# Early tiles in f16 parts, weight halves one expert at a time, a shorter GpSimd prologue, early gates by two transfers

## The chip, the cores and the metric

One NeuronCore of a Trainium2 chip runs the whole kernel. Its engines are TensorE (PE in the profile: matmuls, and PEld for the loading of their weights), VectorE (DVE), ScalarE (ACT), GpSimd (POOL) and SyncE (SP), which here only issues transfers. The metric is the device time of one execution in microseconds. Of the kernel before there are three timed runs, and one execution recorded by the hardware profiler.

## The reference

The block is a gated cross-attention followed by a gated mixture of experts, on 16 x 64 = 1024 tokens of 128 features.

```python
x = x + tanh(g_xattn[0]) * attention(ctx, ctx, layernorm(x), Wk, Wv, bv, Wq, bq, Wo, bo)
x = x + tanh(g_ffn[0]) * ffn(layernorm(x), gate_w, w1, b1, w2, b2)

def ffn(x, gate_w, w1, b1, w2, b2):             # 8 experts, 512 hidden, the best 2 per token
    probs = softmax(einsum('bsd,ed->bse', x, gate_w))
    topk_probs, topk_idx = top_k(probs, 2)
    oh = one_hot(topk_idx, 8)
    h = gelu(einsum('bsd,fed,bske->bskf', x, w1, oh) + take(b1, topk_idx))
    y = einsum('bskf,def,bske->bskd', h, w2, oh) + take(b2, topk_idx)
    return sum(y * topk_probs[..., None], axis=-2)
```

Attention is one head of 128 over 16 sequences of 64 keys. The 2048 choices (1024 tokens times 2) are what the second half of the kernel works through.

## The kernel before, in words

The program is written out by hand for five instruction streams, which meet only at semaphores. Inside a stream everything runs in the order in which it is written: an instruction that waits holds back all that stand behind it on its engine.

**Attention and routing.** The 1024 tokens are eight tiles of 128, taken in four groups of two. A table of times, `TIMES`, sorted into `ORDER`, sets in which order PE, DVE, ACT and POOL take the steps of the groups; the times serve only for sorting. For each group the router picks two experts per token, counts places and finds the row in DRAM to which each choice goes (`slots`). POOL then sends the rows, 16 indirect transfers in all (`send`, L417), into `rows_dram`, where every expert has a region of its own. Ahead of its first send, POOL works through a prologue of constants (L423 to L496).

**The expert tiles.** The choices are worked off in 20 tiles of 128 slots. Tiles 0 to 3 are the early ones: they hold the first 64 slots of each of the 8 experts, two experts to a tile, and don't come through DRAM. `one_hots` (DVE, L1051) builds selection matrices, `gather` (PE, L840) multiplies the normalised rows, split in two f16 halves, with them, and `copy_first` (ACT) takes the sum out. Tiles 4 to 7 are mixed: two experts each, looked up in a table that is made at run time. Tiles 8 to 19 hold one expert each. Tiles 4 to 19 are read back from `rows_dram` (SP, L396 and L402) once all sends have landed; `split_rows` (DVE, L1249 and L1251) splits them in f16 halves, `turn_rows` (PE, L879) transposes them, `copy_rows` (DVE, L1260) takes the result out of PSUM.

**One tile on PE.** `hidden(t)` multiplies with the first weights: early tiles in FP32 (L897), the others as three f16 products, high weights by high rows, high by low, and low by high (L900 to L902). `w1_hi` is made by ACT (`weights_hi`, L594), `w1_lo` by DVE (`weights_lo`, L1213). ACT takes the gelu (L666), and `output(t)` multiplies with the second weights in FP32 (L927). The order on PE is gather, output of the tile before, hidden for an early tile, and hidden(t), output(t - 1), turn_rows(t + 2) from tile 4 on.

**The end.** The results of tiles 0 to 15 go to DRAM by 16 indirect transfers of POOL in the order of the tiles (L510). For tiles 0 to 3 the gate is applied by ACT (`first_gated`, L620), which needs the tile's rows from DRAM for the gate's value and stands in ACT's stream behind the gelu of a later tile. When all 16 have landed, SP reads the results back (L406), and DVE and POOL add them up; tiles 16 to 19 are added by PE from a selection matrix. `keep_clock` (L688) is a run of matmuls that nobody reads, put where PE would otherwise be idle; `CLOCK_FILL` says how many stand where.

## Time and profile before

| what | value |
|---|---|
| three timed runs | 103.09, 103.31 and 103.7 us; median 103.31 |
| the profiled execution | 103.78 us |
| its span, first to last instruction | 102.0 us |
| mean granted TensorE clock | 0.922 of full speed |
| PE / DVE / ACT / POOL busy | 86.3 / 63.0 / 58.3 / 51.3 us |

The span is what the trace covers; the 1.78 us that lie around it are in the time and not in the trace. The busy times are sums over the whole span: no engine is busy throughout, and which one sets the pace changes from stage to stage.

### The profile page before, as it was taken

How to read it: one execution, taken by the hardware profiler on the slowest of the kernel's cores; microseconds unless marked ns; L12 is line 12 of the kernel's file. 1: busy time of each engine (PE TensorE's matmuls, PEld its weight loads, DVE VectorE, ACT ScalarE, POOL GpSimd, SP SyncE). 2: the span in 40 equal slices, each digit the busy share in tenths (PEclk: the TensorE clock that was granted, in tenths of full speed). 3: DMA queues.
4: the chain of work that ended last, by engine and by line, in shares of the span. 5: the costliest groups of instructions: out<-in, count | busy, mean ns of one | idle time of the engine just before them, and what ended most of it. 6: DMA issues, size and time to landing. Idle time of an engine off the chain costs nothing.

```text
span 102.0 us, 3022 instructions
## 1 busy us (share of the span) xinstructions
PE 86.3 (85%) x925; PEld 70.5 (69%) x925; DVE 63.0 (62%) x275; ACT 58.3 (57%) x193; POOL 51.3 (50%) x91
## 2 busy tenths in 40 slices
PE   5949888878996689999997789899999999999500
PEld 1445555743653459989986579778999999999500
DVE  2377759999888948996531202375468885527380
ACT  5356799849668811547666356956666574741000
POOL 6975698308777776740000000373577777700480
PEclk9999999999999855569999958999999999999995
DMA  2999996910111453860222245420110011128315
GB/s 36 328 420 431 431 431 241 289 42 26 55 52 52 124 140 107 249 246 13 58 38 45 52 103 124 90 71 18 40 34 18 26 42 58 46 53 278 113 55 151
DMA packets 11839, 13.32 MB, mean 131 GB/s; under 512 B 1475, under 2 KB 10327, under 8 KB 11568
## 3 DMA queue, kind: packets, MB, share of 16 engines
q1 hardware_dynamic: 10112, 10.59, 31.7%
q0 software_dynamic: 1024, 1.92, 5.8%
q10 hardware_dynamic: 688, 0.61, 2.2%
q8 instruction: 8, 0.13, 0.5%
q14 instruction: 7, 0.06, 0.2%
HBM read 9.03 MB, written 4.29 MB: 131 GB/s over the span
## 4 chain that ended last, share of the span: by engine, by line
PE 29%; POOL 20%; DMA 15%; issue 14%; DVE 12%; SPq 6%; POOLq 1%; ACT 1%; DVEq 0%
POOL dispatched L417 13%; PE bank L927 12%; DMA res<-results 5%; PE bank L900 5%; PE bank L902 4%; DMA x_sb<-in_x 4%; SPq L394 3%; PE bank L901 3%; SPq L396 3%; DMA dispatched<-rows,slot 3%; DMA results<-y_sb,in_rows 2%; POOL results L510 2%; PE bank L879 2%; DMA in_rows<-dispatched 2%; POOL rstd L454 2%
## 5 line engine op out<-in xcount | busy, mean ns | idle before, releaser
L666 ACT ACTIVATE hid<-bank,wp 128x64 f32<-128x64 f32 (+1 forms) x112 | 28.0, 339 | 19.8 <-PE bank L902 12.4
L510 POOL DMA_INDIRECT results<-y_sb,in_rows x16 | 16.2, 1013 | 27.1 <-ACT y_sb L620 23.4
L927 PE MATMUL bank<-w_sb,hid 128*128 (+2 forms) x192 | 23.3, 299 | 0.0
L417 POOL DMA_INDIRECT dispatched<-rows,slot x16 | 16.5, 1032 | 9.1 <-issue 8.2
L927 PEld LDWEIGHTS bank<-w_sb,hid 128*64 128x64 f32 (+1 forms) x192 | 19.9, 178 | 0.2
L900 PE MATMUL bank<-xs_t,w_hi 128*128 128x128 f16 (+1 forms) x80 | 13.9, 215 | 1.3 <-DVE xs_t L1260 1.3
L901 PE MATMUL bank<-xs_t,w_hi 128*128 128x128 f16 (+1 forms) x80 | 13.8, 213 | 0.0
L902 PE MATMUL bank<-xs_t,w_lo 128*128 128x128 f16 (+1 forms) x80 | 13.8, 212 | 0.0
L1260 DVE COPY xs_t<-bank 128x256 f16<-128x256 f16 x16 | 4.6, 290 | 14.2 <-PE bank L879 14.2
L688 PE MATMUL bank<-ones 128*128 128x512 bf16 x38 | 11.6, 423 | 1.2 <-DVE ones L995 1.2
L897 PE MATMUL bank<-xs_f,w_sb 128*128 128x64 f32 x64 | 9.7, 315 | 0.0
L900 PEld LDWEIGHTS bank<-xs_t,w_hi 128*128 x80 | 8.0, 101 | 2.2 <-issue 1.4
L897 PEld LDWEIGHTS bank<-xs_f,w_sb 128*128 128x128 f32 x64 | 9.1, 226 | 0.6 <-issue 0.5
L901 PEld LDWEIGHTS bank<-xs_t,w_hi 128*128 x80 | 8.0, 101 | 0.0
L902 PEld LDWEIGHTS bank<-xs_t,w_lo 128*128 x80 | 7.9, 100 | 0.0
L840 PE MATMUL bank<-hot,rows 128*128 128x128 f16 x64 | 6.2, 264 | 1.3 <-DVE hot L1051 1.2
L1249 DVE CAST parts<-in_rows 128x128 f16<-128x128 f32 x16 | 5.0, 313 | 3.8 <-DMA in_rows<-dispatched 3.8
L688 PEld LDWEIGHTS bank<-ones 128*128 128x128 bf16 x38 | 3.8, 111 | 4.3 <-issue 1.9
L840 PEld LDWEIGHTS bank<-hot,rows 128*128 128x128 f16 x64 | 5.3, 123 | 1.9 <-DVE hot L1051 1.0
L1213 DVE SCALAR_TENSOR_TENSOR w_lo<-w_sb,w_hi 128x512 f16<-128x512 f32 x8 | 5.0, 692 | 2.2 <-ACT w_hi L594 2.2
L569 ACT ACTIVATE rows<-x,nbias,rstd 128x256 f32<-128x256 f32 x8 | 4.4, 593 | 2.0 <-DVE nbias L1120 1.9
L1051 DVE TENSOR_TENSOR hot<-slot_no,pos 128x256 f16<-128x256 f32 (+1 forms) x12 | 5.4, 508 | 0.0
(198 smaller groups left out, 171.0 us busy)
## 6 DMA issues: line engine op xcount, KB each, us to landing
w_sb<-in_w SPq DMA_DIRECT2D x2, 2048.0 KB, 10.7
results<-zeros SPq DMA_DIRECT2D x1, 1024.0 KB, 5.7
w_second<-in_w SPq DMA_DIRECT2D x4, 256.0 KB, 4.3
res<-results SPq DMA_DIRECT2D x4, 256.0 KB, 5.0
in_rows<-dispatched SPq DMA_DIRECT2D x12, 65.0 KB, 2.0
dispatched<-pad_rows SPq DMA_DIRECT2D x9, 65.0 KB, 2.4
in_rows<-dispatched SPq DMA_DIRECT2D x16, 32.5 KB, 2.1
ctx_sb<-in_ctx_t SPq DMA_DIRECT2D x1, 512.0 KB, 4.9
```

The lines of the kernel that those rows point to most:

```text
L417: pool.indirect_dma_start(rows_dram, bass.IndirectOffsetOnAxis(ap=slot[:, t, k:k + 1], axis=0), rows[:, t, k, :], None).then_inc(sent, 16)
L510: pool.indirect_dma_start(results_dram, bass.IndirectOffsetOnAxis(ap=in_rows[:].bitcast(U32)[:, t, TARGET:TARGET + 1], axis=0), y_sb[:, t, ...
L666: mm = act.activation(hid[:, t % HIDS, b, part], hid_ps[h % len(hid_ps)][:, at + part.start:at + part.stop], ACT.Gelu_apprx_tanh, bias=b1[ ...
L688: pe.matmul(to[:, :], ones[:], ones[:, None, :].to_broadcast((P, 4, P)), start=True, stop=True)
L840: mm = pe.matmul(gather_ps[i % 2][:, 0:P], rows_16[:, t, c, :], hot[:, i, t, :, :], start=t == 0 and c == 0, stop=t == TILES - 1 and c == 1)
L897: mm = pe.matmul(to, w1_sb[:, e, f], xs_f[:, t, part], start=True, stop=True)
L900: pe.matmul(to, w1_hi[:, e, f], hi, start=True, stop=False)
L901: pe.matmul(to, w1_hi[:, e, f], lo, start=False, stop=False)
L902: mm = pe.matmul(to, w1_lo[:, e, f], hi, start=False, stop=True)
L927: mm = pe.matmul(to[part, :], hid[:, t % HIDS, b, part], weights, start=False, stop=b == BLOCKS - 1)
L1051: v.tensor_tensor(hot[:, i, a:b, :, :], slot_no[:, None, 2 * i:2 * i + 2, :].to_broadcast(shape), pos[:, a:b, 2 * i:2 * i + 2, None].to_br ...
L1213: v.scalar_tensor_tensor(to[:, q, :], at[:, q, :], WSCALE, hi[:, q, :], ALU.mult, ALU.subtract).then_inc(made_lo, 1)
```

## The change

The changed kernel makes these edits:

- The early tiles use the three f16 products too. `gather` writes the sums of the high and of the low halves into two pieces of PSUM, `copy_first` copies both as f16 (256 columns in place of 128), and `hidden` of an early tile waits for the low weights of its two experts.
- The high weights are made one expert at a time (eight copies of 512 columns in place of four of 1024), five of them further forward in the order; the low weights stand between the selection matrices instead of behind them all.
- On DVE the gates and slots of the last group stand before `locate`, `lanes` and `table` stand later, and the split of tile 6 stands behind the copies of tiles 4 and 5 instead of ahead of them.
- POOL's prologue loses nine instructions: numbers are used as integers where they were copied to FP32, and two pairs of comparisons become one each. The counting matmuls take f16 operands.
- The early tiles' rows from DRAM, needed only for gates and targets, come by two transfers behind tile 7's, in place of eight that took turns with tiles 4 to 7.
- `first_gated(t)` stands behind the gelu of tile t + 6 in place of t + 5.
- Three more matmuls of `keep_clock` follow the last group's ranks.

On DVE, once the last selection matrix of the first early tile is being made, these rows stand in the kernel before (`hot` is the selection matrices, `slot` the rows in DRAM of the last group, `b_16` and `w_lo` low halves of weights):

```order
L1130 SCALAR_TENSOR_TENSOR rows<-exps,tanhs,exp_rec 128x4
L1144 TENSOR_REDUCE slot<-place_k 128x4
L1033 SCALAR_TENSOR_TENSOR b_16<-b_in,b_16 32x128
L1051 TENSOR_TENSOR hot<-slot_no,pos 128x512
L1051 TENSOR_TENSOR hot<-slot_no,pos 128x256 x2
L1051 TENSOR_TENSOR hot<-slot_no,pos 128x512
L1051 TENSOR_TENSOR hot<-slot_no,pos 128x256 x2
L1051 TENSOR_TENSOR hot<-slot_no,pos 128x512
L1051 TENSOR_TENSOR hot<-slot_no,pos 128x256 x2
L1213 SCALAR_TENSOR_TENSOR w_lo<-w_sb,w_hi 128x512 x8
```

In the changed kernel the same stretch of DVE's stream reads (`tile_row`, `tile_experts`, `sel` and `tile_rows` are the table of the further tiles):

```order
L1020 SCALAR_TENSOR_TENSOR b_16<-b_in,b_16 32x128
L1198 SCALAR_TENSOR_TENSOR w_lo<-w_sb,w_hi 128x512 x2
L1037 TENSOR_TENSOR hot<-slot_i,pos 128x512
L1037 TENSOR_TENSOR hot<-slot_i,pos 128x256 x2
L1169 SCALAR_TENSOR_TENSOR tile_row<-bank,place_i 1x20
L1170 TENSOR_SCALAR tile_experts<-bank 1x20
L1172 TENSOR_SCALAR sel<-bank,lane_less 128x20
L1174 TENSOR_SCALAR tile_rows<-tile_row 1x20
L1198 SCALAR_TENSOR_TENSOR w_lo<-w_sb,w_hi 128x512 x2
L1037 TENSOR_TENSOR hot<-slot_i,pos 128x512
L1037 TENSOR_TENSOR hot<-slot_i,pos 128x256 x2
L1198 SCALAR_TENSOR_TENSOR w_lo<-w_sb,w_hi 128x512 x2
```

The slots of the last group have left this stretch (they stand 14 rows ahead of `b_16` now), the table has come into it, and each early tile now has two low weights behind its selection matrices.

Further on in DVE's stream of the kernel before, the first rows from DRAM are split (`parts`, first tile 4, then 5, then 6) and copied (`xs_t`):

```order
L1213 SCALAR_TENSOR_TENSOR w_lo<-w_sb,w_hi 128x512 x8
L1249 CAST parts<-in_rows 128x128
L1251 TENSOR_TENSOR parts<-in_rows,parts 128x128
L1249 CAST parts<-in_rows 128x128
L1251 TENSOR_TENSOR parts<-in_rows,parts 128x128
L1249 CAST parts<-in_rows 128x128
L1251 TENSOR_TENSOR parts<-in_rows,parts 128x128
L1260 COPY xs_t<-bank 128x256 x3
```

In the changed kernel this place on DVE reads:

```order
L1198 SCALAR_TENSOR_TENSOR w_lo<-w_sb,w_hi 128x512 x2
L1238 CAST parts<-in_rows 128x128
L1240 TENSOR_TENSOR parts<-in_rows,parts 128x128
L1238 CAST parts<-in_rows 128x128
L1240 TENSOR_TENSOR parts<-in_rows,parts 128x128
L1246 COPY xs_t<-bank 128x256 x2
L1238 CAST parts<-in_rows 128x128
L1240 TENSOR_TENSOR parts<-in_rows,parts 128x128
L1246 COPY xs_t<-bank 128x256
```

The copies of tiles 4 and 5 no longer stand behind the split of tile 6.

The diff, cut to what the edits above rest on:

```diff
-LAG = 2
+LAG, LATER = 2, 2
+FIRST_LOADS = 4
...
-    W1_HIGH: [14.9],
+    W1_HIGH: [14.9, 14.91, 22.2, 23.6, 28.0, 33.0],
...
-              (RANKS, 2): 2, (X1_T, 3): 3, (ROUTE, 3): 6, (RANKS, 3): 3}
+              (RANKS, 2): 2, (X1_T, 3): 3, (ROUTE, 3): 6, (RANKS, 3): 6}
 W1_LOW_EARLY = 1
-HIGH_PARTS = 4
+HIGH_PARTS = 8
...
-            def load_shared(t):
-                for i in range(2):
-                    half = slice(i * PART, (i + 1) * PART)
-                    if t < EARLY:
-                        at = FIRST_ROW + (2 * t + i) * REGION
-                        sp.dma_start(in_rows[half, t, :], rows_dram[at:at + PART, :]).then_inc(loaded[t], 16)
-                    else:
-                        sp.dma_start(in_rows[half, t, :], rows_dram[bass.ds(first[2 * (t - EARLY) + i], PART), :]).then_inc(loaded[t], 16)
-
-            for t in range(EARLY, SHARED):
-                load_shared(t)
-                load_shared(t - EARLY)
-            for t in range(SHARED, N_TILES):
-                sp.dma_start(in_rows[:, t, :], rows_dram[bass.ds(first[2 * MIXED + t - SHARED], SLOT_TILE), :]).then_inc(loaded[t], 16)
+            regions = rows_dram[FIRST_ROW:PAD_ROW, :].rearrange("(t i r) w -> i r t w", i=2, r=REGION)
+            for t in range(EARLY, N_TILES):
+                if t == EARLY + FIRST_LOADS:
+                    for i in range(2):
+                        sp.dma_start(in_rows[i * PART:(i + 1) * PART, 0:EARLY, :], regions[i, 0:PART, :, :]).then_inc(loaded_first, 16)
+                for part, i in entries(t):
+                    sp.dma_start(in_rows[part, t, :], rows_dram[bass.ds(first[i - EXPERTS], part.stop - part.start), :]).then_inc(loaded[t], 16)
...
-            pool.tensor_copy(slot_no[:], slot_i[:]).then_inc(numbers_set, 1)
...
-            pool.tensor_copy(past[:], past_i[:]).then_inc(numbers_set, 1)
-            pool.tensor_scalar(second[:], lane_i[:], EXPERTS - 0.5, float(EXPERTS), ALU.is_gt, ALU.mult).then_inc(numbers_set, 1)
-            pool.tensor_copy(lane_f[:], lane_i[:]).then_inc(numbers_set, 1)
-            pool.tensor_copy(place_no[:], place_i[:]).then_inc(numbers_set, 1)
-            pool.tensor_copy(edge[:], edge_i[:]).then_inc(numbers_set, 1)
-            pool.wait_ge(numbers_set, 9)
-            for i in range(2):
-                pool.tensor_scalar(after[:, i, :], past[:], EXPERTS * i + 0.5, None, ALU.is_gt).then_inc(numbers_set, 1)
-                pool.tensor_scalar(same[:, i, :], past[:], float(EXPERTS * i), None, ALU.is_equal).then_inc(numbers_set, 1)
-            pool.tensor_tensor(seg_expert[:], lane_f[:], second[:], ALU.subtract).then_inc(numbers_set, 1)
-            pool.tensor_scalar(seg_first[:], second[:], 2.0 * WHOLE / EXPERTS, None, ALU.mult).then_inc(numbers_set, 1)
-            pool.wait_ge(numbers_set, 15)
+            pool.tensor_scalar(after[:], past_i[:], 0.5, None, ALU.is_gt).then_inc(numbers_set, 1)
+            pool.tensor_scalar(same[:], past_i[:], 0.0, None, ALU.is_equal).then_inc(numbers_set, 1)
+            pool.tensor_scalar(seg_first[:], lane_i[:], EXPERTS - 0.5, 2.0 * WHOLE, ALU.is_gt, ALU.mult).then_inc(numbers_set, 1)
+            pool.wait_ge(numbers_set, 3)
+            pool.tensor_tensor(seg_expert[:], lane_i[:], seg_wrap[:], ALU.add).then_inc(numbers_set, 1)
+            pool.wait_ge(numbers_set, 7)
             pool.tensor_scalar(seg_row[:], seg_expert[:], float(REGION // PART), float((FIRST_ROW + PART - PAD_ROW) // PART), ALU.mult, ALU.add).then_inc(numbers_set, 1)
             pool.tensor_scalar(seg_less[:], seg_expert[:], -float(EXPERTS), None, ALU.add).then_inc(numbers_set, 1)
...
-                act.activation(xs_f[:, t, :], gather_ps[t % 2][:, 0:P], ACT.Copy).then_inc(first_ok, 1)
+                act.activation(xs_first[:, t, :, :], gather_ps[t % 2][:, 0:2 * P].rearrange("p (c s) -> p c s", c=2), ACT.Copy).then_inc(first_ok, 1)
...
-                act.wait_ge(loaded[t], loads_of(t))
+                act.wait_ge(loaded_first, 32)
...
-            weights_hi(w1_hi, w1_sb, ld_w1, w1hi_ok, 1)
+            weights_hi(w1_hi, w1_sb, ld_w1, w1hi_ok, 6)
...
-                if t in (1, 2):
-                    weights_hi(w1_hi, w1_sb, ld_w1, w1hi_ok, t + 1)
+                if t == 1:
+                    weights_hi(w1_hi, w1_sb, ld_w1, w1hi_ok, 7)
...
-                if EARLY + 1 <= t < 2 * EARLY + 1:
-                    first_gated(t - EARLY - 1)
+                if EARLY + LATER <= t < 2 * EARLY + LATER:
+                    first_gated(t - EARLY - LATER)
...
-                            mm = pe.matmul(gather_ps[i % 2][:, 0:P], rows_16[:, t, c, :], hot[:, i, t, :, :],
+                            mm = pe.matmul(gather_ps[i % 2][:, c * P:(c + 1) * P], rows_16[:, t, c, :], hot[:, i, t, :, :],
...
-                if t < IN_FP32:
-                    pe.wait_ge(loaded[t], loads_of(t))
-                    pe.transpose(xs_ps[t % 2][:, 0:P], in_f[:, t, 0:P], ident[:]).then_inc(xs_in_ps, 1)
-                else:
-                    pe.wait_ge(parts_ok, t - IN_FP32 + 1)
-                    to = xs_ps[t % 2][:, :].bitcast(F16)
-                    for c in range(2):
-                        mm = pe.transpose(to[:, c * P:(c + 1) * P], parts[:, t % XS, c, :], ident16[:])
-                    mm.then_inc(xs_in_ps, 1)
+                pe.wait_ge(parts_ok, t - EARLY + 1)
+                to = xs_ps[t % 2][:, :].bitcast(F16)
+                for c in range(2):
+                    mm = pe.transpose(to[:, c * P:(c + 1) * P], parts[:, t % XS, c, :], ident16[:])
+                mm.then_inc(xs_in_ps, 1)
 
             def hidden(t):
                 if t < EARLY:
                     pe.wait_ge(first_ok, t + 1)
+                    pe.wait_ge(w1_ok, 2 * t + 2)
                 else:
                     pe.wait_ge(xs_ok, t - EARLY + 1)
-                if t == IN_FP32:
-                    pe.wait_ge(w1_ok, PARTS)
+                xs = xs_first[:, t] if t < EARLY else xs_t[:, t % XS]
                 for b in range(BLOCKS):
                     h = HALVES * t + b // HALVES
                     f = slice(b * P, (b + 1) * P)
@@ -893,13 +883,9 @@
                     for part, i in entries(t):
                         to = hid_ps[h % len(hid_ps)][:, at + part.start:at + part.stop]
                         e = experts[i]
-                        if t < IN_FP32:
-                            mm = pe.matmul(to, w1_sb[:, e, f], xs_f[:, t, part], start=True, stop=True)
-                        else:
-                            hi, lo = xs_t[:, t % XS, 0, part], xs_t[:, t % XS, 1, part]
-                            pe.matmul(to, w1_hi[:, e, f], hi, start=True, stop=False)
-                            pe.matmul(to, w1_hi[:, e, f], lo, start=False, stop=False)
-                            mm = pe.matmul(to, w1_lo[:, e, f], hi, start=False, stop=True)
+                        pe.matmul(to, w1_hi[:, e, f], xs[:, 0, part], start=True, stop=False)
+                        pe.matmul(to, w1_hi[:, e, f], xs[:, 1, part], start=False, stop=False)
+                        mm = pe.matmul(to, w1_lo[:, e, f], xs[:, 0, part], start=False, stop=True)
...
-                    lane_made = lanes()
                     one_hots(0, 0)
+                    gates(g)
+                    slots(g)
                     locate()
                     rows_low(2)
                     one_hots(0, 1)
                     rows_low(3)
                     one_hots(0, 2)
-                    table(lane_made)
-                    gates(g)
-                    slots(g)
                 else:
...
+            lane_made = lanes()
             bias_low()
-            for i in range(1, EARLY):
-                for k in range(len(HOT_CHUNKS)):
-                    one_hots(i, k)
-            for i in range(PARTS):
-                low_weights(i)
+            for i in range(EARLY):
+                if i:
+                    for k in range(len(HOT_CHUNKS)):
+                        one_hots(i, k)
+                if i == 1:
+                    table(lane_made)
+                for e in range(2 * i, 2 * i + 2):
+                    low_weights(e)
...
-            for t in range(EARLY, EARLY + LAG + 1):
-                if t >= IN_FP32:
-                    split_rows(t)
+            for t in range(EARLY, EARLY + LAG):
+                split_rows(t)
             for t in range(EARLY, EARLY + LAG):
                 copy_rows(t)
+            split_rows(EARLY + LAG)
```

## Rows read from the trace of the kernel before

**Rows 1.** The chain of waits, around 54 us: start, length, what.

```profile
53.77 1.95 DMA in_rows<-dispatched
```

**Rows 2.** Timeline of DVE: start, us, instruction, [idle before, releaser].

```profile
36.41 0.41 DVE L1051 TENSOR_TENSOR hot<-slot_no,pos 128x256 f16<-128x256 f32 x1
...
38.89 0.15 DVE L1126 TENSOR_REDUCE exp_sum<-exps 128x2 f32<-128x16 f32 x1
...
39.63 0.28 DVE L1033 SCALAR_TENSOR_TENSOR b<-b_in,b 32x128 f16<-32x128 f32 x1
39.94 3.91 DVE L1051 TENSOR_TENSOR hot<-slot_no,pos 128x512 f16<-128x512 f32 x9
43.76 3.70 DVE L1213 SCALAR_TENSOR_TENSOR w_lo<-w_sb,w_hi 128x512 f16<-128x512 f32 x6
...
56.21 0.48 DVE L1260 COPY xs_t<-bank 128x256 f16<-128x256 f16 x2
```

**Rows 3.** Timeline of PE, 38 to 67 us.

```profile
38.38 3.67 PE L897 MATMUL bank<-xs_f,w_sb 128*128 128x64 f32 x16
...
47.23 1.06 PE L840 MATMUL bank<-hot,rows 128*128 128x128 f16 x16
...
48.30 1.04 PE L927 MATMUL bank<-w_sb,hid 128*64 128x128 f32 x16
...
56.64 0.20 PE L900 MATMUL bank<-xs_t,w_hi 128*128 128x64 f16 x1 [1.27 <-DVE xs_t L1260]
...
58.35 0.20 PE L900 MATMUL bank<-xs_t,w_hi 128*128 128x64 f16 x1
...
59.00 1.95 PE L927 MATMUL bank<-w_sb,hid 128*64 128x128 f32 x16
...
63.64 0.19 PE L900 MATMUL bank<-xs_t,w_hi 128*128 128x64 f16 x1
...
63.90 0.19 PE L900 MATMUL bank<-xs_t,w_hi 128*128 128x64 f16 x1
...
66.74 0.19 PE L900 MATMUL bank<-xs_t,w_hi 128*128 128x64 f16 x1
```

**Rows 4.** Stretches: us, PE busy, granted clock (PEclk), DMA share, GB/s.

```profile
45.00:46.00 1.00, 1.00 (x13) 0.96 0.30 110
...
59.00:60.00 1.00, 1.00 (x12) 0.50 0.37 95
```

**Rows 5.** Timeline of POOL: its indirect transfers.

```profile
22.95 1.24 POOL L417 DMA_INDIRECT dispatched<-rows,slot  x1 [3.92 <-issue]
...
39.87 0.96 POOL L417 DMA_INDIRECT dispatched<-rows,slot  x1 [0.95 <-DVE slot L1144]
...
72.11 1.00 POOL L510 DMA_INDIRECT results<-y_sb,in_rows  x1 [1.35 <-ACT y_sb L620]
...
88.02 0.97 POOL L510 DMA_INDIRECT results<-y_sb,in_rows  x1 [0.30 <-issue]
```

**Rows 6.** Timeline of ACT.

```profile
31.03 1.09 ACT L569 ACTIVATE rows<-x,nbias,rstd 128x256 f32<-128x256 f32 x2 [1.04 <-DVE nbias L1120]
...
43.98 1.05 ACT L594 ACTIVATE w_hi<-w_sb 128x1024 f16<-128x1024 f32 x1
...
70.41 1.14 ACT L666 ACTIVATE hid<-bank,wp 128x128 f32<-128x128 f32 x4 [0.92 <-PE bank L902]
...
72.35 1.14 ACT L666 ACTIVATE hid<-bank,wp 128x128 f32<-128x128 f32 x4 [0.51 <-PE bank L902]
```

**Rows 7.** Waits of SP's queue: who waited for whom, us in total, times, longest.

```profile
SPq L396 <- DMA dispatched<-rows,slot: 2.9, 1, 2.9
```

**Rows 8.** Timeline of SP: transfers issued.

```profile
46.59 1.23 SPq L396 DMA_DIRECT2D in_rows<-dispatched  x2
...
49.29 1.18 SPq L396 DMA_DIRECT2D in_rows<-dispatched  x2
```

**Rows 9.** The page's costliest groups: busy us, mean ns of one.

```profile
L900 PEld LDWEIGHTS bank<-xs_t,w_hi 128*128 x80 | 8.0, 101 | 2.2 <-issue 1.4
```

More of the change, by code:

```diff
@@ L922, in output @@
                     for part, i in entries(t):
-                        if EARLY <= t < SHARED and part.start:
-                            weights = w2_second[:, t - EARLY, f]
+                        if t in MIXED_TILES and part.start:
+                            weights = w2_second[:, t - MIXED_AT, f]
                         else:
```

133 lines of the change are left out of this document (69 added, 64 removed).

## The prediction

> **What bounds the kernel now.** I read the chain of waits first, then the timelines of the engines that it names, then the granted clock. The chain falls into three stretches.
>
> Up to 46 us POOL's 16 sends carry it, and then SP, which issues the loads of the rows one after the other. The chain leaves SP at a load that lands at 55.72 [rows 1]. That is tile 6's, although PE waits for tile 4: DVE splits tiles 4, 5 and 6 ahead of its first copy, and the two copies start at 56.21, right behind the split of tile 6 [rows 2]. PE, idle for 1.27 us, begins tile 4 at 56.64 [rows 3]. This wait is one of order, not of data.
>
> Before it, PE goes through the early tiles: from 38.38 to about 45 us at half of its clock, and the same from 59 to 62 us, behind the idle stretch [rows 3, 4]. The granted clock is 0.96 in the second from 45 us and 0.50 in that from 59 us; these are the two levels of 2.4 and 1.2 GHz. At the lower one 16 matmuls of `output` take 1.95 us, at the higher one 1.04 [rows 3].
>
> From 72 us on POOL carries the chain. The fourth of its 16 result transfers starts at 72.11, the last at 88.02, so the twelve steps between them take 15.91 us, 1.33 each, with 0.30 of gap at the last: POOL is full [rows 5]. Where the fourth starts is set by ACT, which applies the gate of tile 3 behind the gelu of tile 8 (70.41 to 71.55) [rows 6]. What follows the last transfer (its landing, the reading back, the sums) depends on nothing earlier. So the change is worth what it moves the start of the fourth transfer.
>
> **The change, part by part.** *Moving the gates* alone costs. `first_gated(3)` now follows the gelu of tile 9, which starts at 72.35 against 70.41: 1.94 us later in the terms of the tiles [rows 6]. Everything else must be set against this.
>
> *DVE ahead of the early tiles.* The last matrix of tile 0 ends at 36.82. Gates and slots of the last group (38.89 to 39.63, 0.74) come in front of it, `lanes` only changes sides, then `bias_low` (0.31) and two low weights (3.70 / 6 = 0.62 each): 36.82 + 0.74 + 0.31 + 1.24 = 39.11 [rows 2]. PE's first hidden may begin then, 0.7 later than before (38.38). Each later tile needs three matrices (3.91 / 9 x 3 = 1.30) and two low weights (1.24), 2.54 in all, less than PE will need, so DVE hides.
>
> *Early tiles on PE.* A hidden of 24 f16 matmuls of 64 columns: in tile 6, where the queue is full, every third starts 0.087 us after the last (63.64 to 63.90 for nine), 0.029 each, so 0.70 us, and twice that, 1.40, at half clock [rows 3]. In FP32 tile 0 took 3.67. The 64 f16 matmuls of `gather` stay as many. Gather to output is 1.07 (47.23 to 48.30), output 1.04, at half clock 2.0 and 1.95. I take the half clock to last to 45 us as before: hidden(0) 39.15 to 40.55, gather(1) to 42.55, output(0) to 44.5, hidden(1) to 45.45 (0.5 us at half clock, the rest at full). Two more tiles of 1.07 + 1.04 + 0.70 = 2.81 end at 51.1. The turns of tiles 4 and 5 and a copy stand between this and hidden(4); from copy to matmul took 0.43 (56.21 to 56.64), the turns some 0.25 more: 51.8.
>
> *The rows of tiles 4 and 5.* POOL waited 0.95 us for the last group's slots, where a gap without a wait is 0.30 [rows 5]; with the slots in front this goes, and SP's first load moves from 46.59 to 45.94 [rows 8]. SP itself waited 2.9 for the sends, which covers that the table is now made about 2 us later [rows 7]. Four half loads, some 0.7 apart, end with an issue at 48.05, landing 1.95 later [rows 1, 8]; with the split the rows are there by 50.6. PE is the later of the two, but by 0.5 us only.
>
> *The shorter prologue of POOL* I cost at nothing. POOL idled 3.92 us ahead of its first send, none of it for a producer that the profile names [rows 5]. The bounds: no gain, or the first send up to 2 us earlier; of the latter SP could use 0.5, and PE none of it as long as it is the later.
>
> *The high weights one at a time* issue four more ACT instructions, each about half of the 1.05 us of a double one. The gaps in ACT's stream ahead of the rows of a group hide them (1.04 ahead of the last) [rows 6]; without that cover a group is 0.5 later, which POOL's own backlog of sends takes up. The three matmuls of `keep_clock`, the integer operands and the f16 counts fall in waits that `gates` and `slots` now fill: nothing, or some tenths.
>
> *Two transfers for the gates* free SP of six issues. Tile 6 comes some 1.4 and tile 7 some 2.8 us earlier against tile 4; nothing waits for them once tile 6 is out of the copies' way.
>
> *From tile 4 on.* Hidden(4) goes at 0.244 a trio ((58.35 - 56.64) / 7), 1.95 in all, because behind a wait its addresses are worked out one by one; that stays. Then 0.4 of gap, and output(3) at 1.04 in place of 1.95, since PE hardly idles ahead of it, and 0.2 for the turn: hidden(5) at 55.4. A mixed tile at full clock takes 3.10 (63.64 to 66.74), so hidden(6) at 58.5, against 63.64: 5.1 earlier [rows 3]. I take 5.0, since two paths meet closely at 51.
>
> *The sum.* Tiles 5.0 earlier, gates 1.94 later: the fourth transfer and all behind it 3.1 earlier. The span of 102.0 becomes 98.9; with the 1.8 around it the profiled time of 103.78 becomes 100.7. The median of the runs lies 0.47 below that execution: 103.31 - 3.1 = **100.2 us**.
>
> **The rivals.** *The clock takes some of it back.* The half clock could last one tile longer, or fall again at hidden(4) as it did at 59 us. For it: hidden(4) is as thin on PE as it was then, and PE has waits at 35 to 39 us as before. Against it: the idle 1.27 us are gone, and f16 tiles keep PE denser. A second fall costs 1.95 - 1.04 and some tenths, a tile at half clock 1.0 + 0.9 + 0.7, of which the longer stay gives back a part: 1 to 2 us, **101.7**.
>
> *The half clock lasts through hidden(2).* Then gather(2), output(1) and hidden(2) cost 1.0 + 0.9 + 0.7 more and hidden(1) 0.45: 3.0 of the 3.1 are gone and it stays at **103.2**, within 0.5%. The same follows if a load of tile 5 lands 3 us late.
>
> *More than forecast.* The clock returns earlier, the first send comes earlier, and POOL's steps keep to 1.27 instead of 1.33: about 0.6 and 0.7 more, **98.9**.
>
> *Slower: weight loads one after the other.* Every 64 columns bring a weight load of their own, and the trace gives one load a mean of 101 ns [rows 9]. If the loads didn't overlap, a hidden would take 24 x 0.101 = 2.42 in place of 0.70, tile 0 2.42 in place of 1.40: 1.0 + 3 x 1.7 = 6.2 us later, tiles 1.2 later than before, gates 1.94 on top: **106.4**. It decides from the point where the tiles gain less than 1.94, that is where a hidden takes over 1.5 us. Against it: in tile 6 the same trios with the same loads start 0.029 us apart [rows 3].
>
> The Trainium skill's page "TensorE: Matmul & The Clock Gate", section "LDWEIGHTS (loading the stationary operand)", gives a load the number of its columns over 1.2 GHz, whatever the rows. By that, 24 loads of 128 columns would take 2.56 us a tile, and the sum would come to about 107. The trace agrees on the length of one load and not on the pace.
>
> **How the numbers follow.** Forecast 0.60, its own range 99.3 to 101.2; the clock taking some back 0.18; no change 0.08; more 0.08; slower 0.06. Low end 98.8, where the third rival lies; high end 102.6, past the first; what is left out is most of no change and slower. About 0.5% (0.5 us) is what a measurement of this kernel can tell from no change. Faster by more: 0.60 + 0.17 + 0.08 = 0.85; the same 0.08; slower 0.07.
>
> **What would show it.** In the profile after: the copies of tiles 4 and 5 ahead of the split of tile 6, and hidden(4) near 52; early hiddens of 0.7 us at full clock; no second stretch at 0.50; the fourth result transfer near 69 and the last 15.9 later, POOL without waits between them; the first send still near 23. Wrong would be: an early hidden over 1.5 us; PE waiting for low weights in tiles 1 to 3; the last transfer waiting for PE rather than for POOL; or a fourth transfer later than 71.

## The result, and the profile after

The changed kernel takes 104.24 us (median of 20 runs), the kernel before 103.26 beside it: a ratio of 1.012, interval 1.008 to 1.016. It is 1% slower, where 3% faster was forecast. The ratios here and below compare fast executions alone, while the medians take in slow ones too, so a difference between medians of separate batches is rough.

The early tiles do what the prediction says. TensorE's timeline in the changed kernel (start, us, what, [idle before, what ended it]):

```profile
43.60 0.20 PE L886 MATMUL bank<-xs_first,w_hi 128*128 128x64 f16 x1
...
44.31 1.06 PE L834 MATMUL bank<-hot,rows 128*128 128x128 f16 x16
...
49.51 0.20 PE L886 MATMUL bank<-xs_first,w_hi 128*128 128x64 f16 x1
...
53.03 0.40 PE L869 MATMUL bank<-ident,parts 128*128 128x128 f16 x2 [2.65 <-DVE parts L1240]
54.53 0.40 PE L869 MATMUL bank<-ident,parts 128*128 128x128 f16 x2 [1.10 <-DVE parts L1240]
54.82 0.23 PE L886 MATMUL bank<-xs_t,w_hi 128*128 128x64 f16 x1
...
57.23 1.95 PE L913 MATMUL bank<-w_sb,hid 128*64 128x128 f32 x16
```

A `hidden` of an early tile takes 0.71 us (43.60 to 44.31), and the last ends near 50.4, some 4.8 us ahead of before (55.14). Then PE waits 2.65 and 1.10 us for rows. Tile 4 starts at 54.82, against 56.64 in [rows 3]. The granted clock, from the table of stretches, falls again behind this wait as it did in [rows 4] (in each row: the stretch, its length, the busy us and counts of PE, PEld, DVE, ACT and POOL, the granted clock, the DMA share and GB/s):

```profile
45.00:50.00 5.00, 5.00 (x100) 4.00 (x98) 2.19 (x5) 3.54 (x17) 3.04 (x1) 1.00 0.29 96
...
53.00:54.00 1.00, 0.40 (x2) 0.13 (x2) 0.08 (x1) 0.00 (x0) 0.00 (x0) 0.50 0.29 65
```

Why the rows are late stands in GpSimd's timeline, beside [rows 5]:

```profile
21.19 1.24 POOL L412 DMA_INDIRECT dispatched<-rows,slot  x1 [3.82 <-DVE slot L1130]
...
36.73 1.40 POOL L412 DMA_INDIRECT dispatched<-rows,slot  x1 [0.31 <-issue]
38.44 1.12 POOL L412 DMA_INDIRECT dispatched<-rows,slot  x1 [0.30 <-issue]
39.86 0.96 POOL L412 DMA_INDIRECT dispatched<-rows,slot  x1 [0.30 <-issue]
41.12 6.91 POOL L412 DMA_INDIRECT dispatched<-rows,slot  x1 [0.31 <-issue]
...
73.01 0.97 POOL L500 DMA_INDIRECT results<-y_sb,in_rows  x1 [1.70 <-ACT y_sb L610]
...
88.93 0.97 POOL L500 DMA_INDIRECT results<-y_sb,in_rows  x1 [0.31 <-issue]
```

The sends begin 1.76 us earlier, but the 16th takes 6.91 us where most of the others take 0.96, and SP waits for it: its first load goes at 49.72, not at 46.59 [rows 8].

```profile
49.72 5.66 SPq L397 DMA_DIRECT2D in_rows<-dispatched  x8
```

From there everything is late: the fourth result transfer comes at 73.01, 0.90 behind [rows 5], the last one 15.92 us after it as before. That 0.90 is the loss, to within what lies behind the last transfer (13.98 us of the span before, 13.47 after). VectorE's timeline beside the long send:

```profile
37.72 0.28 DVE L1020 SCALAR_TENSOR_TENSOR b<-b_in,b 32x128 f16<-32x128 f32 x1
38.03 1.29 DVE L1198 SCALAR_TENSOR_TENSOR w_lo<-w_sb,w_hi 128x512 f16<-128x512 f32 x2
39.24 1.41 DVE L1037 TENSOR_TENSOR hot<-slot_i,pos 128x512 f16<-128x512 int32 x3
...
40.89 0.15 DVE L1174 TENSOR_SCALAR tile_rows<-tile_row 1x20 int32<-1x20 f32 x1
40.97 1.27 DVE L1198 SCALAR_TENSOR_TENSOR w_lo<-w_sb,w_hi 128x512 f16<-128x512 f32 x2
42.17 1.34 DVE L1037 TENSOR_TENSOR hot<-slot_i,pos 128x512 f16<-128x512 int32 x3
43.44 1.27 DVE L1198 SCALAR_TENSOR_TENSOR w_lo<-w_sb,w_hi 128x512 f16<-128x512 f32 x2
44.65 1.34 DVE L1037 TENSOR_TENSOR hot<-slot_i,pos 128x512 f16<-128x512 int32 x3
45.92 1.27 DVE L1198 SCALAR_TENSOR_TENSOR w_lo<-w_sb,w_hi 128x512 f16<-128x512 f32 x2
```

Twelve instructions with two inputs in SBUF follow each other from 40.97 to 47.19 without a gap. The send ends 0.84 us behind the last of them.

### The profile page after: what moved, and what is told of

The parts are those of the page before. It is cut to its first block, busy times and chain, and to the rows that moved or that the text cites. A ratio compares the mean times of both kernels' runs of the same rounds, so it can differ in the third digit from the quotient of the medians.

```text
span 102.4 us, 3061 instructions
## 1 busy us (share of the span) xinstructions
PE 81.2 (79%) x955; PEld 63.2 (62%) x955; DVE 63.1 (62%) x274; ACT 59.0 (58%) x197; POOL 55.1 (54%) x82
## 3 DMA queue, kind: packets, MB, share of 16 engines
q0 software_dynamic: 1024, 1.92, 5.8%
## 4 chain that ended last, share of the span: by engine, by line
PE 28%; DMA 21%; DVE 14%; POOL 13%; issue 9%; ACT 7%; SPq 3%; POOLq 1%; DVEq 0%
PE bank L913 12%; POOL dispatched L412 8%; DMA dispatched<-rows,slot 8%; PE bank L886 5%; DMA res<-results 4%; DMA x_sb<-in_x 4%; PE bank L888 4%; PE bank L887 3%; DMA results<-y_sb,in_rows 3%; PE bank L869 3%; DMA in_rows<-dispatched 2%; DVE parts L1238 2%; POOL results L500 2%; POOL rstd L451 2%; ACT probs L548 2%
## 5 line engine op out<-in xcount | busy, mean ns | idle before, releaser
L412 POOL DMA_INDIRECT dispatched<-rows,slot x16 | 22.3, 1392 | 8.4 <-DVE slot L1130 4.1
L913 PEld LDWEIGHTS bank<-w_sb,hid 128*64 128x64 f32 (+1 forms) x192 | 19.2, 172 | 0.9 <-ACT hid L656 0.4
L678 PE MATMUL bank<-ones 128*128 128x512 bf16 x41 | 12.7, 433 | 1.2 <-DVE ones L982 1.2
L869 PE MATMUL bank<-ident,parts 128*128 128x128 f16 x32 | 4.8, 236 | 4.4 <-DVE parts L1240 4.4
L834 PE MATMUL bank<-hot,rows 128*128 128x128 f16 x64 | 5.4, 243 | 1.6 <-DVE hot L1037 1.6
L869 PEld LDWEIGHTS bank<-ident,parts 128*128 128x128 f16 x32 | 2.6, 100 | 6.0 <-DVE parts L1240 5.0
L926 PE MATMUL bank<-y,whose 128*128 128x128 f16 x64 | 4.4, 219 | 1.7 <-DVE y L1255 1.7
L834 PEld LDWEIGHTS bank<-hot,rows 128*128 128x128 f16 x64 | 4.4, 111 | 2.0 <-DVE hot L1037 2.0
L1037 DVE TENSOR_TENSOR hot<-slot_i,pos 128x256 f16<-128x256 int32 (+1 forms) x12 | 5.6, 501 | 0.0
L901 PE MATMUL bank<-b,sel 128*64 128x128 f16 (+1 forms) x28 | 4.7, 234 | 0.7 <-issue 0.6
```

Source lines behind the costliest of these rows:

```text
L412: pool.indirect_dma_start(rows_dram, bass.IndirectOffsetOnAxis(ap=slot[:, t, k:k + 1], axis=0), rows[:, t, k, :], None).then_inc(sent, 16)
L678: pe.matmul(to[:, :], ones[:], ones[:, None, :].to_broadcast((P, 4, P)), start=True, stop=True)
L834: mm = pe.matmul(gather_ps[i % 2][:, c * P:(c + 1) * P], rows_16[:, t, c, :], hot[:, i, t, :, :], start=t == 0 and c == 0, stop=t == TILES ...
L869: mm = pe.transpose(to[:, c * P:(c + 1) * P], parts[:, t % XS, c, :], ident16[:])
L913: mm = pe.matmul(to[part, :], hid[:, t % HIDS, b, part], weights, start=False, stop=b == BLOCKS - 1)
L1037: v.tensor_tensor(hot[:, i, a:b, :, :], slot_i[:, None, 2 * i:2 * i + 2, :].to_broadcast(shape), pos[:, a:b, 2 * i:2 * i + 2, None].to_bro ...
```

## The experiments

| kernel | us, median | ratio to before (interval) | last send, us |
|---|---|---|---|
| changed | 104.24 | 1.012 (1.008 to 1.016) | 6.91 |
| w2_late | 106.29 | 1.024 (1.008 to 1.040) | 6.91 |
| hots_first | 104.91 | 1.017 (1.006 to 1.028) | 6.92 |
| dve_pause | 101.52 | 0.980 (0.967 to 0.993) | 0.96 |
| gates_at_5 | 102.19 | 0.987 (0.973 to 1.000) | 6.92 |
| two_waits | 104.55 | 1.008 (1.001 to 1.016) | 6.91 |
| hot_f32 | 104.59 | 1.008 (1.001 to 1.014) | 6.91 |
| two_waits_g5 | 101.28 | 0.975 (0.964 to 0.987) | 6.91 |
| after_phase | 104.53 | 1.010 (1.001 to 1.020) | 6.63 |
| table_gap | 101.20 | 0.968 (0.961 to 0.974) | 0.96 |
| pause_g5 | 99.13 | 0.953 (0.946 to 0.961) | 0.96 |
| pause_g4 | 98.16 | 0.946 (0.941 to 0.952) | 0.95 |

**What holds the send up.** First suspect: the 1 MB of second weights, issued at 41.54. `w2_late` moves it behind the loads of tiles 4 and 5:

```diff
-            for u in range(at_mixed, at_mixed + 2 * MIXED, LOADS):   # ahead of the wait for the sends
+                if t == EARLY + 2:                                   # in the loop over the loads
+                    for u in range(at_mixed, at_mixed + 2 * MIXED, LOADS):
```

> The changed kernel with one move on SP: the four 256 KB transfers of second weight tables (issued at 41.54 to 43.79 there) are issued only after the loads of tiles 4 and 5. Theory A (GpSimd's last send is kept waiting by VectorE's unbroken run of two-input instructions in SBUF, 38.03 to 47.19): the last send still takes 6 to 7 us and SP's first load stays near 49.5; the time stays near 104, or rises by up to 1 us because the second weights now land about 7 us later. Theory B (the last send waits for room in the DMA engines, which the 1 MB fills): the last send takes 0.96 us like the others, SP's first load comes near 44.5, tile 4 starts near 51.5 and the time falls to about 101.

The send took 6.91 us all the same: theory B falls. (The time rose by 2 us to 106.29, more than the expectation allowed; the cause isn't shown.) `dve_pause` lets VectorE wait, ahead of expert 2's low half, for a signal behind the last send:

```diff
                 if i == 1:
                     table(lane_made)
+                    v.wait_ge(all_sent, 1)
...
+            pool.engine_nop().then_inc(all_sent, 1)
             limit = pool.to_reg(SLOTS - 1)
```

> The changed kernel with one wait more: before the low halves of experts 2 to 7 VectorE waits until GpSimd has issued its last send (a signal right behind it). Theory A (VectorE's unbroken run holds the send up): the last send, at 41.1, takes about 1 us, VectorE loses 1.1 us, SP's first load comes near 44.5 in place of 49.72, tile 4 starts near 51.5 in place of 54.82, and the time falls to about 101 (3 us below the changed kernel). Theory B (the 1 MB of second weights holds it up): the last send still takes 6 us or more, VectorE's run is pushed back behind it by as much, and the time rises above 106. Theory C (the send stalls for another reason, such as the earlier start of the sends): as B.

The send took 0.96 us and the time fell from 1.012 of before to 0.980 (2.7 us between the medians): theory A holds. (In the profiled execution all sends began some 3 us late, the first at 24.28, so SP's first load, at 49.52 and not near 44.5, tells nothing.) In `hots_first` VectorE makes all one-hots ahead of the low halves of experts 2 to 7.

```diff
+            for e in range(2):
+                low_weights(e)
...
+            for e in range(2, EXPERTS):
+                low_weights(e)
```

> The changed kernel with VectorE's order changed: after the low halves of experts 0 and 1 come all nine one-hot instructions (4 us), then the low halves of experts 2 to 7. Theory A1 (only the low halves, two fp32 and f16 inputs, keep GpSimd out): the last send, at 41.1, lies beside one-hots and takes about 1 us, SP's first load comes near 44.5, the time falls to about 101. Theory A2 (any unbroken run of two-input instructions does): the last send ends with VectorE's run as now, near 48, and the time stays near 104. Theory B (the second weights' 1 MB): as A2.

6.92 us, to 0.84 behind the end of that run too. So the low halves alone aren't to blame (A1 falls).

**The gates.** `gates_at_5` undoes that part of the change alone.

```diff
-LAG, LATER = 2, 2
+LAG, LATER = 2, 1
```

> The changed kernel with LATER = 1: ScalarE gates the early tiles in the passes of tiles 5 to 8 again, not 6 to 9; all else as changed. If the fourth result transfer (73.01, its gate at 72.32) still sets the end, the gates come one pass earlier, the fourth near 69.7, and the last transfer with them: the time falls by 2 to 2.7 us to about 101.7. If the time falls by under 0.5 us, something other than the gates sets the end by now, such as the pace of the later tiles or the landing of the early rows (issued at 55.43).

Between the medians this is 2.05 us less. `two_waits` and `two_waits_g5` (below), run side by side, differ by 3.27 in the same way. In the traces SP's first load and the fourth transfer lie 20.47 us apart here (51.03 and 71.50) and 23.29 in the changed kernel: 2.8 less. The term was real, and larger than 1.94; the part on why the prediction was wrong says where the rest comes from.

**Why it didn't happen before.** There four sends lay beside nine one-hots and six low halves, at 0.96 to 0.99 us. Two differences of form were tried first, and neither counts:

```diff
                 v.wait_ge(dve, pos_made[GROUPS - 1])
+                v.wait_ge(numbers_set, 2)                 # two_waits; taken out in before_one_wait
-                v.tensor_tensor(hot[...], slot_i[...],
+                v.tensor_tensor(hot[...], slot_no[...],   # hot_f32
```

> The changed kernel with one line put back: each one-hot instruction on VectorE waits for a second, long satisfied semaphore (numbers_set), as in the kernel before, where sends beside nine one-hots took 0.96 to 0.99 us. Theory W (back-to-back VectorE instructions with two SBUF inputs keep GpSimd's send out, and a second wait ahead of an instruction opens a gap that lets it in): the last send, from 41.1, is let in at the first one-hot after the low halves (42.2) and ends near 43.0 in place of 48.03; SP's first load comes near 45.5 in place of 49.72; the time falls to about 101.5. Theory T (the operand type decides: int32 one-hots and low halves hold the port, fp32 one-hots don't): the last send still takes 6.9 us and the time stays near 104.

> The changed kernel with the one-hots fed from fp32 slot numbers, as before the change (converted once by VectorE near 3.4 us, where it is idle), still with one wait each. Theory T (int32 operands make the one-hots hold GpSimd out): the last send, stuck from 41.1 behind two low halves, is let in at the first one-hot (42.2) and ends near 43.0; the time falls to about 101.5. Theory W (the second wait made the gap, the type has no part in it): the last send takes 6.9 us as in the changed kernel, and the time stays near 104.

> The kernel before with one line taken out: the one-hots' second wait (numbers_set, which VectorE has waited for already, with a higher count, in counting the tiles). Theory W: the sends that started at 41.14, 42.44 and 43.71 beside the one-hots are no longer let in between them; the first of these ends only behind VectorE's run (near 48.3), the last two follow (near 50.8), SP's first load comes near 53 in place of 46.59, and the time rises by 4 to 6 us to about 108. Theory T: nothing changes, sends 0.96 to 0.99 us and the time 103.3.

The send took 6.91 us in the first two. In the third the sends beside the one-hots took 0.96 to 1.00, and the time was 104.66 (ratio 1.004, 0.999 to 1.010). W and T fall. (`two_waits_g5` adds the earlier gates to the first; it is `gates_at_5` over again in its sends.)

Next, luck: the old sends, 1.26 us apart, could have met a boundary between two one-hots each time. A useless instruction shifts one send:

```diff
+                if (t, k) == (6, 1):          # (7, 1) in after_phase
+                    pool.iota(scratch[:], [[1, 320]], base=0, channel_multiplier=0)
```

> The kernel before with one useless GpSimd instruction (an iota of 128x320, about 0.36 us) put between its 13th and 14th send, so that the 14th starts near 41.5, inside a one-hot (41.21 to 41.82), and no longer 0.05 us ahead of a boundary between two of them. Theory P (the send needs VectorE's shared path for a moment early on; it gets in when that moment falls on a boundary between two instructions, and otherwise waits, often to the end of the unbroken run; the kernel before had three lucky moments, pitch 1.26 us of the sends against 1.27 us of the one-hots): the 14th send takes about 6.7 us, to 48.2, the 15th and 16th follow to 50.7, SP's first load comes near 53 in place of 46.59 and the time rises by 4 to 6 us, to 108. Against P: the sends take 0.96 to 1.6 us, each let in at the next boundary, and the time moves by under 0.7 us.

> The changed kernel with the same useless instruction between its 15th and 16th send, so that the 16th starts near 41.5 in place of 41.12, just ahead of the boundary between the low halves of experts 2 and 3 (41.57). Theory P: it is let in there and ends near 42.5 in place of 48.03; SP's first load comes near 45 in place of 49.72, and the time falls by 2 to 3 us to about 101.5. If the shift misses the boundary by more than 0.1 us, P lets it stay stuck to 48.0. Against P: stuck to 48.0 although it starts within 0.1 us ahead of the boundary.

The first went against it. The second can't decide: its send came at 41.39, some 0.14 us ahead of the boundary (near 41.53, halfway between 40.93 and 42.14, where the two low halves and the next one-hot begin), and a miss of over 0.1 us was allowed to stay stuck. GpSimd in before_phase:

```profile
40.86 0.43 POOL L419 IOTA scratch<- 128x320 int32 x1
41.47 1.32 POOL L420 DMA_INDIRECT dispatched<-rows,slot  x1 [0.18 <-issue]
```

The shifted send lost 0.36 us and was let in at the next boundary (104.47 us, ratio 1.005); that of the changed kernel, brought to 41.39, was stuck for 6.63. Then the place, in three kernels whose single times (104.6, 105.2 and 105.0 us) say little. hots_first_f32 is hots_first with the one-hots of before, before_int is before_phase with those of the change, and before_mixed is before_phase with the low halves in between:

```diff
-                v.wait_ge(numbers_set, 2)                 # before_int; put in by hots_first_f32
-                v.tensor_tensor(hot[...], slot_no[...],
+                v.tensor_tensor(hot[...], slot_i[...],    # the other way round in hots_first_f32
...
+                for e in range(2 * i - 2, 2 * i):         # before_mixed
+                    low_weights(e)
                 for k in range(len(HOT_CHUNKS)):
                     one_hots(i, k)
```

> The changed kernel with VectorE's order as in hots_first and the one-hots in their old form (fp32 slot numbers, two waits), so that the last send, near 41, starts inside a run of six such one-hots, as the 14th did in before_phase. Theory F (the form of the instructions decides: a run of old one-hots opens at each boundary): the send is let in at the next boundary and takes 1.0 to 1.5 us in place of 6.92. Theory E (the place decides: the last send, or one that comes just behind the four short instructions of the table, is shut out till the run ends): 6.9 us, to about 47.8.

> The kernel before with the useless GpSimd instruction ahead of the 14th send (as in before_phase, where the send took 1.32 us) and with the one-hots in their new form: int32 slot numbers and one wait. Theory F: the 14th send is shut out to the end of VectorE's run, near 47.4, and takes 6.7 us; the time rises to 108. Theory E: it takes 1.3 us as in before_phase, and the time is 104.

> The kernel before with the useless GpSimd instruction ahead of the 14th send (as in before_phase) and with VectorE's low halves set between the one-hots, two ahead of each three, as the change has them. Theory M (the mixing of the two kinds decides): the 14th send, from 41.5 inside a one-hot, is shut out until VectorE next stops (near 45, where it waits for ScalarE's third high half), some 4 us in place of 1.32. Theories F and E: let in at the next boundary, 1.0 to 1.6 us.

6.92, 1.32 and 1.25 us: neither form nor mixing counts, the place does. `before_gap` holds the 13th send of the kernel before back into the run:

```diff
+            if t == STARTS[GROUPS - 1]:
+                pool.wait_ge(hot_ok, len(HOT_CHUNKS) + 1)
```

> The kernel before with its 13th send held back until the fourth one-hot is made, so that VectorE's unbroken run (nine one-hots, six low halves, from about 39.9) begins while GpSimd sends nothing; before, the 13th send had started 0.07 us ahead of the run. Theory S (a run that starts between two sends shuts GpSimd out to its end; one that starts beside a send opens at its boundaries): the 13th send, from about 40.7, takes some 7.5 us, to 48.3, the last ends near 52, SP's first load comes near 55 in place of 46.59, the time rises by 6 to 8 us. Theory L (only the last send is ever shut out): all four take 0.96 to 1.4 us, SP's first load comes 0.8 us later, the time rises by under 1 us.

The four took 1.30, 0.97, 0.97 and 1.50 us, each let in at the next boundary. S falls; and the last send is not special, since it too came in the midst of the run, so L doesn't explain the changed kernel either. (The sends resumed at 41.57, later than worked out; its single time is 106.48 us.)

What was left is what stands ahead of the run. In the changed kernel the table's last instruction (40.89, 0.15) overlaps the first low half by 0.07 us; the open runs begin 0.03 us behind `b`. `table_gap` makes a gap there:

```diff
                 if i == 1:
                     table(lane_made)
+                    v.wait_ge(table_ok, 3)
```

> The changed kernel with one wait more on VectorE: the low half of expert 2 waits until the last of the table's four short instructions has finished (a signal of its own that it has at hand), which leaves a gap of some 0.05 us where the two overlapped by 0.07. Theory V (a one-input instruction such as the table's last takes the path that VectorE and GpSimd share, and VectorE gives it back only at its first idle moment; every run that shut a send out followed such an instruction without a gap, and every run that let sends in began behind a gap): the last send, from 41.1, is let in at the next boundary (41.7) and takes 1.0 to 1.6 us, SP's first load comes near 45.5 in place of 49.72, and the time falls by 2 to 3 us to about 101.5, for 0.1 us of VectorE. Against V: the send takes 6.9 to 7.0 us as before, and the time stays at 104.

VectorE and GpSimd in table_gap:

```profile
41.30 0.15 DVE L1174 TENSOR_SCALAR tile_rows<-tile_row 1x20 int32<-1x20 f32 x1
41.49 1.36 DVE L1198 SCALAR_TENSOR_TENSOR w_lo<-w_sb,w_hi 128x512 f16<-128x512 f32 x2
```

```profile
41.53 0.96 POOL L412 DMA_INDIRECT dispatched<-rows,slot  x1 [0.30 <-issue]
```

A gap of 0.04 us gave 3 us (104.24 to 101.20). But the send came only 0.04 us behind the start of an instruction, where the changed kernel's came 0.15 behind it (41.12 and 40.97). `gap_phase_g4` keeps the gap and shifts the send further in (and gates at tiles 4 to 7):

```diff
+                if (t, k) == (7, 1):
+                    pool.iota(scratch[:], [[1, 320]], base=0, channel_multiplier=0)
...
+                    v.wait_ge(table_ok, 3)
...
-LAG, LATER = 2, 2
-FIRST_LOADS = 4
+LAG, LATER = 2, 0
+FIRST_LOADS = 2
```

> table_gap with the useless iota of after_phase ahead of the 16th send, so that the send asks some 0.35 us into the low half of expert 2, not within 0.1 us of its start as in table_gap; and with the gates in the passes of tiles 4 to 7 and the early rows loaded behind tiles 4 and 5, as in pause_g4. Theory V (the gap behind the table's instructions opens the run): the send is let in at the next boundary and takes 1.1 to 1.4 us, SP's first load comes near 46, the time is 98 to 98.7. Theory N (in table_gap the send was only lucky to come at a boundary): it is shut out to the end of VectorE's run, 6.3 to 6.7 us, SP's first load comes near 50 and the time is 100.5 to 102.

GpSimd and VectorE in it, and VectorE in after_phase, which differs there by the gap alone:

```profile
40.97 0.43 POOL L414 IOTA scratch<- 128x320 int32 x1
41.58 1.43 POOL L415 DMA_INDIRECT dispatched<-rows,slot  x1 [0.18 <-issue]
```

```profile
41.05 0.38 DVE L1177 TENSOR_SCALAR tile_rows<-tile_row 1x20 int32<-1x20 f32 x1
41.46 1.29 DVE L1201 SCALAR_TENSOR_TENSOR w_lo<-w_sb,w_hi 128x512 f16<-128x512 f32 x2
```

```profile
40.86 0.39 DVE L1177 TENSOR_SCALAR tile_rows<-tile_row 1x20 int32<-1x20 f32 x1
40.93 1.27 DVE L1201 SCALAR_TENSOR_TENSOR w_lo<-w_sb,w_hi 128x512 f16<-128x512 f32 x2
```

The send came 0.12 us behind the start of the low half, not 0.35 as expected, and in both kernels 0.14 to 0.15 behind the end of `tile_rows`. It lost 0.47 us, to the boundary between the two low halves near 42.07, and not 5.67 as in after_phase (6.63 us): V holds in that the gap opens the run, and N falls. The times spread from 97.25 to 100.36, so the verdict rests on these rows. They show more: `tile_rows` takes 0.38 in place of 0.15 and ends 0.03 behind GpSimd's iota, and 0.39 in after_phase likewise (its iota: 40.80, 0.42). So this small one-input instruction waits for GpSimd: it uses something that the two share.

**The best version.** Pause and earlier gates together:

```diff
-LAG, LATER = 2, 2
+LAG, LATER = 2, 1     # pause_g5; in pause_g4 LATER = 0 and FIRST_LOADS = 2
```

> The changed kernel with VectorE's pause behind the last send (2.6 us gained alone) and LATER = 1 (2.0 gained alone). If both lie on one chain, from SP's first load through the gates to the result transfers, they add: about 99.5. If the early rows' landing (58.2 in the changed kernel) or ScalarE's gates hold the transfers then, only the larger counts: 101.5.

> As pause_g5, but the gates in the passes of tiles 4 to 7 (LATER = 0) and the early rows loaded behind the rows of tiles 4 and 5 (FIRST_LOADS = 2). The fourth result transfer comes one pass earlier still (2 to 2.7 us). If the transfers, 1.28 us apart, still set the end, the time falls to about 97.5; if the pace of the later tiles on TensorE (about 2 us each) sets it by then, it stays within 1 us of pause_g5; if ScalarE waits for the early rows ahead of the second GELU pass, the tiles lose up to 2 us and it is slower than pause_g5.

They add: 99.13 and 98.16 us, both ahead of either kernel. In pause_g4 the transfers no longer set the end. GpSimd waits 0.62 to 0.92 us ahead of each of the last four, where in pause_g5 0.30 lies between them. What it waits for follows TensorE, which the chain of waits names:

```profile
70.20 0.95 PE bank L914 x8
71.15 0.11 PE bank L870 x2
71.99 0.95 PE bank L914 x8
```

```profile
83.40 0.97 POOL L501 DMA_INDIRECT results<-y_sb,in_rows  x1 [0.91 <-DVE y_sb L1254]
```

TensorE's tiles of 1.79 us (70.20 to 71.99) set the end now.

## Why the prediction was wrong

**The step that failed** is "SP's first load moves from 46.59 to 45.94". It took each send as 0.96 us wherever it lay, and the gaps of VectorE as room to be filled at no cost. Filling them put the table's instructions flush against the low halves, and that shut out the last send for 5.95 us. The load came 3.78 late against the forecast, tile 4 3.0 (54.82 for 51.8). The clock fell once more, `output(3)` cost 1.95 (0.91 more), and tile 5 came 3.9 late (59.29 for 55.4). Tile 5 itself took 2.48 where 3.10 was allowed, so tile 6 came 3.3 late (61.77 for 58.5) and the gelu of tile 8 3.2 (68.61, for 70.41 less 5.0).

**A term that was too small** makes up the rest: the gates, at 1.94. Behind them the changed kernel shows, on ACT, VectorE and GpSimd:

```profile
68.61 1.14 ACT L656 ACTIVATE hid<-bank,wp 128x128 f32<-128x128 f32 x4 [0.94 <-PE bank L888]
71.31 1.14 ACT L656 ACTIVATE hid<-bank,wp 128x128 f32<-128x128 f32 x4 [1.27 <-PE bank L888]
```

```profile
68.31 1.72 DVE L1238 CAST parts<-in_rows 128x128 f16<-128x128 f32 x1
```

```profile
68.91 1.04 POOL L504 IOTA token_i<- 128x1024 int32 x1
```

The gelu of tile 9 starts 2.70 us behind that of tile 8, not 1.94. VectorE's split of tile 10 took 1.72 us where others take 0.22, and ended 0.08 behind an iota that GpSimd makes after its second result transfer; TensorE waited 0.63 us for that split. With the gates one pass later the iota falls one pass later too. In table_gap, dve_pause and two_waits, which have the late gates, TensorE waits 0.62 to 0.63 us at this place; in gates_at_5, two_waits_g5 and pause_g5, which have the early ones, it doesn't, and the two gelus are 1.94 apart (in the last two the iota holds up an earlier tile's split, 1.78 and 1.72 us, for which TensorE doesn't wait). So 3.2 of the tiles and 0.8 of the gates are the miss: the fourth transfer came at 73.01 for 69.0, and the time is 104.24 for 100.2. The prediction's own sign of being wrong, a fourth transfer later than 71, is there.

**The other steps, once the send is let in,** mostly hold in pause_g5. TensorE, SP and GpSimd there:

```profile
52.01 0.20 PE L887 MATMUL bank<-xs_t,w_hi 128*128 128x64 f16 x1 [0.23 <-DVE xs_t L1248]
54.39 1.07 PE L914 MATMUL bank<-w_sb,hid 128*64 128x128 f32 x16
55.39 0.29 PE L870 MATMUL bank<-ident,parts 128*128 128x128 f16 x2
58.18 0.28 PE L870 MATMUL bank<-ident,parts 128*128 128x128 f16 x2
```

```profile
45.91 6.56 SPq L397 DMA_DIRECT2D in_rows<-dispatched  x8
```

```profile
66.85 1.00 POOL L501 DMA_INDIRECT results<-y_sb,in_rows  x1 [1.35 <-ACT y_sb L611]
```

- SP's first load: 45.94 forecast, 45.91. That is luck: the forecast had it wait for the sends, which end at 42.06 here. What it waits for is the table (`tile_rows` ends at 41.03) and SP's own issues behind that.
- Tile 4: 51.8, 52.01. `output(3)`: 1.04, 1.07, at full clock. VectorE's copies of tiles 4 and 5 (51.58) come ahead of the split of tile 6 (52.81). Tiles 5 and 6: 55.4 and 58.5 forecast; they start at 55.51 and 58.30, right behind the start of the two turns (55.39 and 58.18).
- The fourth transfer at 66.85, with gates one pass earlier; 1.94 later is 68.8 for "near 69", but with the 2.70 of the late gates it is 69.6.
- In table_gap, the change with nothing but the gap, they hold less well:

```profile
46.75 6.17 SPq L397 DMA_DIRECT2D in_rows<-dispatched  x8
```

```profile
70.38 0.97 POOL L500 DMA_INDIRECT results<-y_sb,in_rows  x1 [1.70 <-ACT y_sb L610]
```

- There TensorE waits 0.80 us for tile 5's rows, the granted clock falls to 0.50 again, and `output(3)` costs 1.95: the rival in which the clock takes some back came true with the send let in. In gap_phase_g4, with a wait of 1.08, it is 1.95 too.
- The time of the change with the send let in is 0.968 of before (table_gap, 0.961 to 0.974) or 0.980 (dve_pause, 0.967 to 0.993). Of the 103.31 that the forecast starts from, these are 100.0 and 101.2 us, at the forecast or 1.0 above it. In table_gap the number is met by luck, since two of its steps, the full clock and the gates' 1.94, were not.

**Smaller misses.** The prologue "at nothing" was wrong: the first send came at 21.19, near the bound of 2 us; it still brought SP nothing, which in pause_g5 waits 1.8 us for the table and none for the sends. The half clock ended near 42.6 in the changed kernel and near 44.8 in pause_g5, where 45 was taken. "From 72 us on POOL carries the chain" was read from the gaps of 0.30: the chain of waits in the kernel before names TensorE's tiles up to 85.00 us and GpSimd only from 85.40 on, so the two came in together.

**The rivals.** None named this; the clock's second fall, which the first one has, came on top of it. "A load of tile 5 lands 3 us late" has the right place and size, without the mechanism, and stood at no change with 0.08. The slower one fell: an early `hidden` starts a matmul each 0.029 us beside loads of 0.1.

The Trainium skill's page "SBUF — State Buffer", section "Who interferes with whom", says that a VectorE instruction with two SBUF inputs contends with a GpSimd instruction that reads SBUF, that `copy`, `cast` and `tensor_scalar` can take both shared ports when their operands meet certain conditions, and that whoever issues second is blocked until the first is done. It also says that a probe showed no `tensor_tensor` stalling a DMA, and marks the reason as inferred. The traces agree that `tile_rows` waits for GpSimd (0.38 for 0.15) and the split of tile 10 too (1.72 for 0.22). They differ in that sends do wait for `TENSOR_TENSOR` (0.36 us in before_phase, to the next boundary), and on the length: 5.95 us over twelve instructions, not one. The rule on two inputs would still have made a rival: it speaks against a change that closes VectorE's gaps beside sends.

What stays open: how the hold passes from the table's instruction to the twelve behind it, and whether the gap counts or the wait that makes it (each added gap came from a wait that VectorE had to sit out; the long satisfied one of two_waits did nothing). The two other sends that missed a boundary (36.00 in the kernel before, 1.66 us; 36.73 in the changed one, 1.40) also lay in a run flush behind short instructions, but the second was let in at a short instruction, with no gap.

## What to carry to other kernels

When a change fills an engine's gaps, look at what another engine did beside them: GpSimd's indirect transfers need moments of VectorE's that no wait in the profile names, and a duration is only fixed in the company that it was measured in. A gap of 0.04 us behind a short one-input instruction, made by a wait on its own signal, was worth 3 us here. And a delay that is put in for cover (the gates one pass later) is to be priced alone: it cost 2.0 to 3.3 us by the medians, where 1.94 was forecast.

## What the runs showed of the hardware

- A send (0.96 us) beside VectorE's two-input instructions is let in at the next boundary between two of them, at a cost of 0.00 to 0.54 us, where their run begins behind a gap of 0.03 us or more; where it begins flush behind a short `TENSOR_SCALAR`, it waited 5.67 to 5.96 us, to the end of the run, in nine kernels.
- Type of the operands, a second wait, the order of the two kinds and whether it was the last send made no difference.
- A `TENSOR_SCALAR` of 1x20 took 0.38 us in place of 0.15 beside a GpSimd iota and ended 0.03 behind it, in two kernels. A `CAST` of 128x128 took 1.72 us in place of 0.22 in the changed kernel and 1.63 in the one before, and ended 0.08 and 0.09 behind a GpSimd iota of 1.04 us.
